# Head of a routed feed-forward stage: when weights are split, stored and subtracted, and how tokens are ranked

## What is computed

```
x = x + 0.5 * ffn2(norm(x))     # "f": 2 experts, top 1, silu(gate)*up, 1024 hidden
x = x + attention(norm(x))      # "a": 16 heads of 16, causal
x = x + 0.5 * ffn2(norm(x))     # "f" again, same weights
x = x + 0.5 * ffn8(norm(x))     # "m": 8 experts, top 2, gelu, 1024 hidden, biases
x = x + mixer(norm(x))          # "s": state space mixer
x = x + 0.5 * ffn8(norm(x))     # "m" again
```

## Time and profile before

| | us |
|---|---|
| median of three runs | 994.5 (992.1 to 997.3) |
| profiled execution | 990.16 |
| its span | 988.3 |
| first stage "f" | 0 to about 152 |
| attention | to about 333 |
| second "f" | to about 452 |
| first "m" | to about 632 |
| mixer | to about 805 |
| second "m" | to the end |

### The profile page before, as it was taken

One profiled execution on the slowest core, in us unless ns is written; L12 is line 12 of the kernel. 1 busy time (PEld: TensorE's weight loads), 2 busy tenths in 40 slices (PEclk: granted clock), 3 DMA queues, 4 the chain that ended last, 5 costly groups with the idle time before them and its releaser, 6 DMA issues.

```text
span 988.3 us, 21269 instructions
## 1 busy us (share of the span) xinstructions
PE 845.4 (86%) x7784; PEld 551.6 (56%) x7785; DVE 615.4 (62%) x1132; ACT 428.9 (43%) x990; POOL 337.2 (34%) x400
## 2 busy tenths in 40 slices
PE   3089988978888789998989999897889879999995
PEld 2046553423333336664689999544344444999993
DVE  5635646678993436654646565676798746555655
ACT  6434435136767515444244444367211152544440
POOL 2212114050000211112344553224888632555530
PEclk9999989989999879997799999999999997999997
DMA  8326622531104214422487664300000003666644
GB/s 292 130 86 213 220 73 75 174 109 48 27 20 172 78 32 144 131 94 92 163 335 242 239 226 155 100 1 1 0 1 0 1 30 115 252 242 238 226 156 142
DMA packets 46296, 125.38 MB, mean 127 GB/s; under 512 B 10202, under 2 KB 23467, under 8 KB 40207
## 3 DMA queue, kind: packets, MB, share of 16 engines
q0 software_dynamic: 13392, 67.96, 19.6%
q1 hardware_dynamic: 26698, 49.36, 15.2%
q10 hardware_dynamic: 6132, 7.05, 2.2%
HBM read 97.28 MB, written 26.71 MB: 125 GB/s over the span
## 4 chain that ended last, share of the span: by engine, by line
PE 57%; DVE 13%; DMA 9%; ACT 8%; POOL 6%; issue 6%; SPq 1%; ACTq 0%; DVEq 0%; POOLq 0%
PE psum L567 16%; PE psum L540 12%; PE psum L526 7%; PE psum L1347 3%; DMA stage<-in_w 3%; DVE mem L1472 2%; PE psum L114 2%; POOL mem L2137 2%; POOL mem L2133 2%; PE psum L513 1%; DMA mem<-xn_dram,mem 1%; PE psum L1900 1%; PE psum L1844 1%; DVE mem L312 1%; DMA max_dram<-mem 1%
## 5 line engine op out<-in xcount | busy, mean ns | idle before, releaser
L567 PE MATMUL psum<-mem 128*128 x1536 | 180.9, 275 | 3.2 <-DVE mem L808 1.9
L567 PEld LDWEIGHTS psum<-mem 128*128 128x128 f16 x1536 | 147.4, 98 | 24.4 <-issue 4.3
L540 PE MATMUL psum<-mem 128*128 128x128 f16 x2208 | 132.0, 220 | 0.0
L916 POOL DMA_INDIRECT y_dram<-mem x64 | 63.5, 993 | 194.5 <-DVE mem L824 194.5
L658 ACT ACTIVATE mem<-psum,mem 128x128 f32<-128x128 f32 x368 | 105.0, 369 | 54.3 <-PE psum L540 52.8
L540 PEld LDWEIGHTS psum<-mem 128*128 128x128 f16 x2208 | 128.1, 98 | 0.7
L911 POOL DMA_INDIRECT mem<-xn_dram,mem x64 | 66.7, 1042 | 120.5 <-PE psum L513 92.4
L1432 ACT ACTIVATE mem<-psum 128x512 f32<-128x512 f32 (+1 forms) x160 | 79.9, 552 | 54.3 <-PE psum L1327 35.5
L526 PE MATMUL psum<-mem 128*128 x432 | 100.3, 390 | 2.2 <-issue 2.2
L114 PE MATMUL psum<-ones 128*128 128x512 f16 x312 | 97.9, 440 | 0.6 <-issue 0.6
L1472 DVE TENSOR_REDUCE mem<-psum 128x2 f32<-128x1024 f32 (+2 forms) x96 | 87.6, 950 | 15.8 <-PE psum L1293 8.7
(11 more groups left out here) (246 smaller groups left out, 1382.1 us busy)
## 6 DMA issues: line engine op xcount, KB each, us to landing
stage<-in_w SPq DMA_DIRECT2D x32, 512.0 KB, 4.0
w_rows<-mem SPq DMA_DIRECT2D x8, 1024.0 KB, 7.6
xn_dram<-mem ACTq DMA_DIRECT2D x32, 128.0 KB, 1.7
mem<-y_dram SPq DMA_DIRECT2D x16, 256.0 KB, 5.2
mem<-in_w_gate SPq DMA_DIRECT2D x4, 512.0 KB, 6.7
mem<-in_w_up SPq DMA_DIRECT2D x4, 512.0 KB, 10.6
mem<-in_w_down SPq DMA_DIRECT2D x4, 512.0 KB, 14.0
mem<-y_dram SPq DMA_DIRECT2D x16, 128.0 KB, 3.4
```

The lines of the kernel that those rows point to most:

```text
L540: ins = eng.matmul(c.bank(2 * p + j // half)[:, j % half * P:(j % half + 1) * P], mats[q][:, l, k, j * P:(j + 1) * P], x[:, p, k, :], star ...
L567: ins = eng.matmul(c.bank(6)[:, 0:D], a[:, 0 if gated else p, q * half + j, :], w[:, at], start=(i == 0), stop=(i == 3 * CF - 1))
L916: eng.indirect_dma_start(c.y_dram[:, :], bass.IndirectOffsetOnAxis(ap=yidx[:, b:b + 1], axis=0), yo[:, b % 2, :], None).then_inc(s_ys[b % ...
```

## The change

It does the following. In the first stage the low part of the third matrix (w_down) is subtracted on DVE behind the inputs of the first two blocks (`weights_late`), the blocks wait for the first two matrices alone, and the second layer of the first block waits for the third (`second_ready`). `split0` goes: the four attention matrices become the first four chunks of `split1`, which now has 21 chunks in the same 8 steps (2, 3, 2, 3, 3, 2, 3, 3). Two chunks of a step stay where they were, a third moves behind the step's other work on ACT and DVE. Quarter 0 of w1 is stored between the first stage and the attention, quarters 1 to 3 behind the attention's last `max_rows`. In the norm, TensorE makes the router logits of the tiles that are ready ("f": six of eight tiles; "m": the first bank, in place of two of the three idle products of the last three tiles). The ranks are made with products over all tiles at once (8 in "f", 16 in "m"). The one-hot matrices are made by 2 wide instructions from f16 numbers. The last expert's comparison and two instructions of the block experts go. ACT runs one-column activations ahead of time, so that its function table is loaded early.

```diff
@@ layernorm_stage: act, pe
+        if table is not None:
+            eng.activation(c.spent[:, 0:1], c.ln_consts[:, 0:1], table)
...
+            worked = between(eng, i) if between is not None else 0
             if "idle_bank" in src:
-                keep_awake(c, eng, src["idle_bank"], 3)
+                keep_awake(c, eng, src["idle_bank"], 3 - min(worked, 2))
@@ moe_stage
+    def router_between(eng, i):
+        if i == 4:
+            for ready in W["router_ready"]:
+                eng.wait_ge(*ready)
+        if gated:
+            if i >= 4:
+                for n in ((0, 1, 2) if i == 4 else (i - 2,)):
+                    router_tile(eng, n)
+            return 0
+        if i < 5:
+            return 0
+        eng.wait_ge(*L["lo"](NT // 2))
+        ins = router_half(eng, 0, range(2 * (i - 5), 2 * (i - 4)))
+        if i == NT - 1:
+            ins.then_inc(s_hid.sem, 1)
+        return 2
...
-        for t in range(NT):
-            out = c.bank(5)[:, NE + t * E:NE + (t + 1) * E]
-            todo = [(c.before16, k, t) for k in range(TOPK)] + [(c.ones16, k, u) for u in range(t) for k in range(TOPK)]
-            for i, (m, k, u) in enumerate(todo):
-                ins = eng.matmul(out, m[:, :], mk[:, k, u, :], start=(i == 0), stop=(i == len(todo) - 1))
+        ranks = c.bank(5)[:, NE:2 * NE].rearrange("p (t e) -> p t e", e=E)
+        for k in range(TOPK):
+            ins = eng.matmul(ranks, c.before16[:, :], mk[:, k, :, :], start=(k == 0), stop=False, skip_group_check=True)
+        for u in range(NT - 1):
+            for k in range(TOPK):
+                ins = eng.matmul(ranks[:, u + 1:NT, :], c.ones16[:, :], mk[:, k, u, :].unsqueeze(1).to_broadcast([P, NT - 1 - u, E]),
+                                 start=False, stop=(u == NT - 2 and k == TOPK - 1), skip_group_check=True)
@@ second
+            else:
+                for ready in W["second_ready"]:
+                    eng.wait_ge(*ready)
@@ act
+        if weights_act is None:
+            eng.activation(c.spent[:, 1:2], c.ln_consts[:, 0:1], ACT.Silu if gated else ACT.Gelu)
...
             block_h(b, p)
             if meanwhile is not None:
-                meanwhile["act"](eng, b)
+                meanwhile["act"](eng, b, False)
             block_act(b + 1, 1 - p)
             if x:
                 block_x(b + 2, p)
+            if meanwhile is not None:
+                meanwhile["act"](eng, b, True)
@@ dve
-        eng.tensor_scalar(ebi[:, :], ebf[:, :], float(E - 1), None, ALU.min).then_inc(s_eb.sem, 1)
         if not gated:
-            link(eng.tensor_scalar(spare[:, :], ebf[:, :], float(E - 1), float(P), ALU.min, ALU.mult))
-            eng.tensor_scalar(widx[:, :], spare[:, :], c.row_spare[:, :], float(1 + TOP2 * T), ALU.add, ALU.subtract).then_inc(s_wi.sem, 1)
-            eng.wait_ge(*s_wi(1))
+            eng.tensor_scalar(widx[:, :], ebf[:, :], float(P), c.row[:, :], ALU.mult, ALU.add).then_inc(s_wi.sem, 1)
+        eng.tensor_copy(ebi[:, :], ebf[:, :]).then_inc(s_eb.sem, 1)
...
-        for i in range(KT):
-            eng.tensor_scalar(oh[:, i, :], c.iota_p[:, :], pcol[:, i // NT, i % NT:i % NT + 1], None, ALU.is_equal)\
-                .then_inc(s_oh.sem, 1)
+        columns = pcol[:, :, :].rearrange("p k t -> p (k t)")
+        for i in range(2):
+            part = slice(i * KT // 2, (i + 1) * KT // 2)
+            eng.tensor_tensor(oh[:, part, :], c.iota16[:, 0:P].unsqueeze(1).to_broadcast([P, KT // 2, P]),
+                              columns[:, part].unsqueeze(2).to_broadcast([P, KT // 2, P]), ALU.is_equal).then_inc(s_oh.sem, 1)
...
             block_y(b, p, first_use)
+            if meanwhile is not None:
+                meanwhile["dve"](eng, b, True)
...
         block_x(0, 0)
         block_x(1, 1)
+        if weights_late is not None:
+            weights_late(eng)
@@ program
-        split0 = split_weights(c, mat_jobs, stage, "act", "dve", after=first["done"](first["count"]))
         W0 = dict(gh=rg_h, gl=rg_l, router_ready=[first["done"](1)], first=[(gate_h, gate_l), (up_h, up_l)],
-                  second=(down_h, down_l), block_ready=[first["done"](first["count"])], first_time=True, idle=8, bias_part=None)
+                  second=(down_h, down_l), block_ready=[first["done"](3)], second_ready=[first["done"](first["count"])], first_time=True, idle=8, bias_part=None)
-        split1 = split_weights(c, [(A["rw1"], flat(rr_h), flat(rr_l)), (A["w1"], w1_h, w1_l)], stage,
-                               after=split0["done"](split0["count"]))
+        split1 = split_weights(c, [*mat_jobs, (A["rw1"], flat(rr_h), flat(rr_l)), (A["w1"], w1_h, w1_l)], stage,
+                               after=first["done"](first["count"]))
...
+            def part(b, late):
+                chunks = chunks_of(split["count"], b)
+                return chunks[2:] if late else chunks[:2]
...
-                for part in range(2):
-                    if i == 2 + 4 * (part + 1):
-                        store_w1(eng, part)
                 split1["load"](eng, i)
...
-                progs.append(dict(sync=store_b1))
+                progs.append(dict(sync=lambda eng: (store_b1(eng), store_w1(eng, 0))))
@@ attention_stage: sync, result
-        store_w1(eng, 2)
-        store_w1(eng, 3)
+        for i in range(1, 4):
+            store_w1(eng, i)
...
-                order=[GROUPS[s][t] for t in range(HALF) for s in range(2)], ready=lambda i: s_xd(i + 1), combine=[], idle_bank=5,
+                order=[GROUPS[s][t] for t in range(HALF) for s in range(2)], ready=lambda i: s_xd(i + 1), combine=[], idle_bank=4,
```

More of the change, by code:

```diff
@@ L114, in keep_awake, with layernorm_stage @@
         eng.matmul(c.bank(bank), c.ones16[:, :], wide, start=True, stop=True)
-def layernorm_stage(c, src, XN, stored=None, lead=True):
+def layernorm_stage(c, src, XN, stored=None, lead=True, between=None, table=None):
     s_st = c.sem("ln_st", NT)
@@ L307, in act, with low, moe_stage @@
             eng.activation(hi, raw[:, i, :], ACT.Copy).then_inc(s_hi.sem, 1)
-    def dve(eng):
-        for i, (src, hi, lo) in enumerate(mats):
-            eng.wait_ge(*s_hi(i + 2))
-            eng.tensor_tensor(lo, raw[:, i, :], hi, ALU.subtract).then_inc(s_lo.sem, 1)
-    return dict(sync=sync, router_dve=router_dve, act=act, dve=dve, done=s_lo, count=1 + len(mats))
-def moe_stage(c, src, E, TOPK, NB, gated, W, region, meanwhile=None, weights_act=None, weights_dve=None, weights_sync=None):
+    def low(eng, i):
+        src, hi, lo = mats[i]
+        eng.wait_ge(*s_hi(i + 2))
+        eng.tensor_tensor(lo, raw[:, i, :], hi, ALU.subtract).then_inc(s_lo.sem, 1)
+    return dict(sync=sync, router_dve=router_dve, act=act, low=low, done=s_lo, count=1 + len(mats))
+def moe_stage(c, src, E, TOPK, NB, gated, W, region, meanwhile=None, weights_act=None, weights_dve=None, weights_late=None, weights_sync=None):
     XN = region.take([NT, D], F32)
@@ L330, in stored, with router_tile, router_half @@
         eng.dma_start(c.xn_dram[1 + t * P:1 + (t + 1) * P, :], XN[:, t, :]).then_inc(s_xs.sem, 16)
-    L = layernorm_stage(c, src, XN, stored, W["bias_part"] is None)
     order = src["order"]
+    def router_tile(eng, n):
+        t = order[n]
+        eng.wait_ge(*L["lo"](n + 1))
+        tok = slice(t * P, (t + 1) * P)
+        i = 0
+        for k in range(KD):
+            for a, b in ((c.XTh, W["gh"]), (c.XTh, W["gl"]), (c.XTl, W["gh"])):
+                ins = eng.matmul(c.bank(5)[:, t * E:(t + 1) * E], a[:, k, tok], b[:, k, :],
+                                 start=(i == 0), stop=(i == 3 * KD - 1))
+                i += 1
+        return ins
+    ROUTER = [(k, a, b) for k in range(KD) for a, b in (("r1h", c.XTh), ("r1l", c.XTh), ("r1h", c.XTl))]
+    def router_half(eng, s, steps):
+        tok = slice(s * BANK, (s + 1) * BANK)
+        for i in steps:
+            k, a, b = ROUTER[i]
+            ins = eng.matmul(c.bank(s), W[a][:, k, :], b[:, k, tok], start=(i == 0), stop=(i == len(ROUTER) - 1))
+        return ins
+    def router_between(eng, i):
[14 more added lines that the diff above has]
+        return 2
+    L = layernorm_stage(c, src, XN, stored, W["bias_part"] is None, router_between, None if gated else ACT.Gelu)
     NE = NT * E
@@ L345, in moe_stage @@
     slotf = region.take([TOPK, NT], F32)
-    pcol = region.take([TOPK, NT], F32)
+    pcol = region.take([TOPK, NT], F16)
     sbase = region.take([TOPK, NT], F32)
+    sbase16 = region.take([TOPK, NT], F16)
     full = region.take([NT, E], F32)
@@ L353, in moe_stage @@
     ends = region.take([E], F32)
-    ebc = region.take([NB, E], F32)
+    ebc = region.take([NB, E - 1], F32)
     ebf = region.take([NB], F32)
@@ L367, in moe_stage @@
     oh = region.take([KT, P], F16)
-    eqb = region.take([KT, NB], F32)
+    eqb = region.take([KT, NB], F16)
     idb = region.take([KT, NB], F16)
@@ L1024, in l1_weights @@
     stage_ = dict(sync=load_cb, act=bias_act, dve=bias_halves, load_w2=load_w2)
```

(17 more changed lines are left out.)

59 lines of the change are left out of this document (23 added, 36 removed).

## The result

The changed kernel takes 965.7 us (median of 4 runs, 963.8 to 966.5) against 993.5 for the kernel before in the same set (4 runs, 992.1 to 997.3): a ratio of 0.9725, 95% interval 0.968 to 0.977. The profiled execution took 966.48 us, span 964.7, against 990.16 and 988.3: 23.7 us less, where the sum of the prediction had 24.2. Some runs of these kernels fall in a slower state of the chip, and those more than 1.5% above the fastest of the same kernel are left out of every median and ratio in this document.

What follows compares the result with a forecast made beforehand. TensorE's own steps bound the blocks, behind waits in the first stage's head. Gains of 19.5 (first stage) + 0.9 + 2 x 1.9 = 24.2 us off 990.16 gave 966.0 profiled, median 970, range 962 to 979.

Steps and rivals of the forecast that it cites:

- Head of the first stage: Ahead of block 0, two subtractions, then the second gather's held descriptors: first layer at 39.1, 13.0 us earlier.
- Steps: First stage's eight block steps, five with three chunks: steps 4, 5 and 7 stall 0.35 us each, 1.0 in all.
- The rival that chunks bind the steps: First stage: every three-chunk step loses 1.25 us, last second layer stays cold; 16.8 us gained in all, 978; chance 0.14.
- stalls fall from 5.4 to 1.0: First stage's steps: with stores away from the loads, TensorE's stalls shrink, a gain of 4.4 us.
- Tail: First stage, last transposition to end of last second layer: that layer runs warm, 2.1 us gained, between 0 and 2.6.
- Stores: Moved w1 stores around the attention: cost 0; quarters 1 to 3 have 12 us of cover ahead of `load_w2`.
- a sign of being wrong: Listed outcomes against the forecast, among them an attention stage longer than before; no size given.
- Second "f": Head of that stage: earlier router products and wide one-hots gain 0.9 us, between 0.3 and 1.4.
- Each "m": Head of each such stage: router 1.0, links and width 0.3, one-hots 0.6, together 1.9 us gained, between 1.0 and 3.4.
- turn-taking or not: One-hots in "m": gain 1.0 us, less 0.8 if POOL's multiplication and DVE alternate; half of that, 0.4, was taken.
- rival 2: Wide one-hots at half time and without turns: 1.2 us more in each "m", 0.3 in each "f", 967; chance 0.08.
- Tables: ACT's early activations: second "m" table load of 1.28 us goes, counted 0; a rival said they move no table.

Runs made afterwards that it cites:

- the controls: The changed kernel itself, unaltered, run again in the second and third sets: medians 974.2 and 973.8 us, ratios to the kernel before 0.969 and 0.976.
- TensorE kept awake: Changed kernel plus a wait and 16 idle products ahead of block 0, 8 behind its first layer, more around the lists: 974.8 us, ratio 0.975.

## Why the prediction was right

**Head of the first stage: 13.0 predicted, 13.1 measured**, by the path it named: subtractions to 35.4, held descriptors, data at 38.0, first layer at 38.99 against 39.1. The step that rested on two rows only, that POOL is held until the running subtraction ends, is now shown by changing the instruction's length alone: 2.65 and 3.79 us beside instructions of 4.4, 1.20 and 1.72 beside instructions of 1.15. The Trainium skill (SBUF — State Buffer, section SBUF: two separate sides) says that the port pair of Vector and GpSimd is locked for a whole instruction, but for the writing of descriptors it names only Vector's two-port modes. Here subtractions with two inputs held it, and the measurement decides. Of the 13.1, the third subtraction is 3.3 and the attention weights the rest, since undoing both moved the first layer by 13.5.

**Steps: 1.0 predicted, 1.0 measured**, in steps 4, 5 and 7 as named: 0.35, 0.28 and 0.30, and 0.06 in step 6. The rival that chunks bind the steps is real, but under other conditions: it needs the stores between the loads (10.9 us) or the third chunk ahead of the gate (11.2 us), and the change has neither.

**The step that failed is "stalls fall from 5.4 to 1.0" as the whole of the steps' account.** It took step 0 at 8.95, as it was before, and the first layer at its old length. Both depend on where the low clock falls. The first layer gained 0.87 (7.75 to 6.88) and step 0 lost 1.74 (10.63, over the 8.89 that the sum counts for a step), neither in the sum. The two belong together: in the eleven traces of the changed kernel and its variants without idle products in this wait, step 0 of the first stage took 10.6 wherever the first layer took up to 7.41, and 8.95 wherever it took 7.58 or more. In the second "f" it is the same: 10.6 behind a first layer of 5.35, and 8.95 behind one of 7.04 or more. So a stretch at 1.2 GHz fell either in the first layer or in the one behind the wait, and a fast first layer alone is no gain.

**Tail: 2.1 predicted, 2.44 measured** (7.54 to 5.10), its last second layer warm. This term is in part luck: in two of the traces, one of them a control, that layer took 4.46 and 4.47, which takes back 1.65. (The prediction took the second "f"'s last transposition at 440.67, which is its second half; it starts at 440.50. That moves 0.17 from the tail to the steps and not the sum.) Together 13.10 + 0.87 + 4.40 - 1.74 + 2.44 = 19.1, against 19.5.

**Stores: 0, right, with less cover than named.** The last six issues ran from 289.32 to 295.54, the DMA engines at full rate until about 306, and `load_w2` began at 315.17: 9 us, not 12. The attention stage came out 0.9 longer, which the text had listed as a sign of being wrong. Among the three traces of the unaltered changed kernel that stage differs by 1.7, so the 0.9 can't be laid to the stores. With two of the six stores and quarter 0 back between the chunk loads the stage was no shorter (189.5 against 187.9), which speaks against them; no run took them all out of the attention. That stays open.

**Second "f": 0.9 predicted**, 0.59 for the router and 0.26 for the one-hots measured; the 0.2 for the first stage's router was wrong, it is 0. The whole stage gained 0.8, though its first layer took 5.35 instead of 7.04: step 0 took 10.6 instead of 8.95.

**Each "m": 1.9 predicted, 2.1 measured** in the head of the second. The router half gave 0.83 (1.0 predicted); the links from the first reduction to the one-hots 0.33 (8.28 to 7.95; 0.3 predicted); the one-hots 0.95, where 0.6 was put as the middle of turn-taking or not. Turns are taken (shown above), yet the full 0.95 came, because only 0.6 of VectorE's time is lost to them. The wide form ran 1.18 us for 1024 columns, as long as a subtraction with a 32-bit input of that width, so rival 2 is out. The doubled speed of the Trainium skill's tier table (VectorE: DVE Perf Modes) is not seen with a repeated operand.

**Tables.** The prediction counted 0 for the early activations and left open whether they move a table load. In the second "m" they do: the load of 1.28 us at 842.15 is gone from the blocks, and the stage's three loads stand ahead of its lists (780.31, 798.13 and 800.05). In the first stage one still stands at the first silu (39.15).

That the sum came within 0.6 us of the span's 23.6 is partly luck: the first "m" gained 3.7, of which 2.2 lies in the one step named under the controls (6.48 instead of 8.72), and in the controls that step was as long as before or longer. Attention and mixer lost 0.9 each.

**The median came out better than the sum.** Between the two profiled executions lie 23.7 us, between the medians 27.8, and in the sets of the controls 30.0 and 29.8. So the change seems to be worth more than the 24.2 of the sum, though no more than its range (16 to 31 us) allows. Where the 4 to 6 us more are won is not shown, since those sets hold no trace of the kernel before.

## What to carry to other kernels

Work that only prepares for later belongs between the steps of a loop bound by another engine, if two things are counted: the loads that feed it must not share their time with bulk stores, and of several pieces in a step the last must stand behind the work that the next step waits for. Either of the two, left out here, cost 11 us and would have eaten most of the 13 of the head. And a part is best measured by its own stretch of the trace: the whole time of the unaltered kernel moved by up to 13 us within one set.

## What the runs showed of the hardware that I had not expected

Behind a wait of 2.4 us TensorE ran its next products in part at 1.2 GHz in some traces and not in others: behind the same wait [2.37 <-DVE mem L842] L558 took 6.81, 7.03 and 5.34 us, the last behind a first layer that had itself run long (8.02). Eight idle products in the wait (1.89 us) removed it in both "f". The same products hurt where they start cold: twelve took 5.28 us, where at the high level they take about 2.7 (estimate from the 1.89 of eight).

The granted clock doesn't tell all: the windows from 40 to 44 us of the changed kernel show it at 1.00, while TensorE had 7 products in the first two of these microseconds, as many as at 0.50 in the window from 50 to 52, and 11 in the next two.

```profile
40.00:42.00 2.00, 2.00 (x7) 0.65 (x5) 2.00 (x1) 0.43 (x1) 0.00 (x0) 1.00 0.21 66
42.00:44.00 2.00, 2.00 (x11) 0.92 (x10) 1.92 (x1) 0.00 (x0) 0.00 (x0) 1.00 0.00 0
```

A faster head can be lost to a DMA queue: in "m" gathers are issued between slab loads and land late. With TensorE kept awake the third block's gather in the second "m" landed 5.8 us after its issue; in the first "m" the gather of the fifth or sixth block took 9.8 to 10.5 in the three traces of the changed kernel. A gather of the second "f" took 2.93. Blocks that start earlier wait longer for them.
